# Channels in blocks of 128 and 64 instead of 96 and 96, and an expert stage that alternates up and down products

## The reference

```python
h = tok(x)                                  # sin/cos features of 3*192 inputs, times W -> (4, 512, 192)
h = concat([cls_tok, h], axis=1)            # (4, 513, 192)
h = h + attn(layernorm(h))                  # 8 heads with relative positions, then an MLP 192 -> 384 -> 192
h = h + ffn(layernorm(h))

def ffn(x):
    # "attention" over channels: 12 heads of 16 channels, softmax(q @ k) over channels
    a = (w @ v).reshape(B, N, 192) @ W2_w + W2_b
    x = layernorm_global(a + x)             # one mean and one variance over all images, tokens and channels
    scores = x @ r_w + r_b                  # 8 experts; softmax of the mean over tokens, top 2 per image
    hmid = gelu_tanh(x @ fc_w[e] + fc_b[e]) # 192 -> 768
    m = sum over the 2 experts of gate * (hmid @ proj_w[e] + proj_b[e])
    return layernorm_global(m + x)
```

## Time and profile before

| | us |
|---|---|
| median of three runs | 1060.34 |
| lowest, highest | 1058.44, 1064.05 |
| profiled execution | 1069.61 |
| its span, first to last instruction | 1067.8 |
| PE busy | 937.8 (88%) |
| VectorE busy | 716.2 (67%) |
| ScalarE busy | 659.7 (62%) |
| expert products, first start to last end | 905.7 to 1052.5 |

### The profile page before, as it was taken

The page is one execution under the profiler, slowest core; times in us unless marked ns, Lnnn a source line. Parts: engine busy times, 40 slices in busy tenths (PEclk is TensorE's granted clock), DMA queues, the critical chain, the costliest instruction groups (busy, mean ns, idle before and its releaser), DMA issues. The chain is left out here.

```text
span 1067.8 us, 20398 instructions
## 1 busy us (share of the span) xinstructions
PE 937.8 (88%) x6627; PEld 827.4 (77%) x6627; DVE 716.2 (67%) x1655; ACT 659.7 (62%) x1196; POOL 154.4 (14%) x210
## 2 busy tenths in 40 slices
PE   5999999999977998899889988996978984899996
PEld 5899999999965776677568666764967763899996
DVE  7899979899444865597558655974753436465555
ACT  5767747667436875687569756975344423575653
POOL 1000000000010432043204320444600000000000
PEclk9999999999978998999999999998588997899997
DMA  7012100199514971487148714972001112413101
GB/s 251 21 31 82 36 30 34 34 147 143 83 34 130 274 225 50 119 267 224 52 119 273 225 45 119 284 232 69 29 1 30 30 45 75 133 48 96 48 0 59
DMA packets 81547, 112.93 MB, mean 106 GB/s; under 512 B 10669, under 2 KB 42426, under 8 KB 81482
## 3 DMA queue, kind: packets, MB, share of 16 engines
q1 hardware_dynamic: 81482, 112.16, 39.4%
HBM read 61.30 MB, written 47.67 MB: 102 GB/s over the span
## 5 line engine op out<-in xcount | busy, mean ns | idle before, releaser
L390 PE MATMUL psum<-w,feat 128*128 128x192 f32 x960 | 168.5, 331 | 13.9 <-ACT feat L320 10.3
L390 PEld LDWEIGHTS psum<-w,feat 128*128 128x128 f32 x960 | 157.1, 192 | 14.7 <-issue 10.2
L605 POOL TENSOR_SCALAR a_scores<-a_scores,a_inv 112x514 f32<-112x514 f32 (+1 forms) x160 | 112.6, 705 | 295.3 <-DVE a_inv L954 295.1
L939 DVE CUSTOM_DVE_ANT_0 a_scores<-psum,a_bias 112x514 f32<-112x514 f32 (+1 forms) x160 | 109.9, 689 | 49.7 <-PE psum L678 41.6
L827 ACT ACTIVATE a_scores<-a_scores,a_least 112x514 f32<-112x514 f32 (+1 forms) x160 | 116.6, 728 | 13.6 <-DVE a_least L939 12.9
L408 PE MATMUL psum<-w_parts,parts 128*128 128x384 f32 x368 | 113.0, 372 | 3.4 <-DVE parts L222 2.9
L691 PE MATMUL psum<-ident,a_scores 112*112 112x112 f32 (+1 forms) x800 | 102.7, 260 | 13.4 <-DVE a_probsT L949 8.3
L320 ACT ACTIVATE feat<-turn 128x1024 f32<-128x1024 f32 (+1 forms) x60 | 58.4, 974 | 85.7 <-DVE turn L205 52.5
L678 PE MATMUL psum<-a_kh,a_q 128*112 128x258 f32 (+1 forms) x320 | 101.2, 337 | 7.4 <-DVE a_q L909 3.8
L691 PEld LDWEIGHTS psum<-ident,a_scores 112*112 112x112 f32 (+1 forms) x800 | 78.0, 137 | 35.0 <-POOL a_scores L605 18.7
L632 PE MATMUL psum<-h1T,place 96*128 (+3 forms) x320 | 89.7, 420 | 13.5 <-DVEq L902 6.9
(11 more groups left out here) (271 smaller groups left out, 1759.4 us busy)
## 6 DMA issues: line engine op xcount, KB each, us to landing
shear<-a_pos SPq DMA_DIRECT2D x128, 224.9 KB, 3.9
a_bias<-shear SPq DMA_DIRECT2D x128, 224.4 KB, 3.9
shear<-zero SPq DMA_DIRECT2D x20, 448.9 KB, 17.1
e_fc<-in_e_fc_dram SPq DMA_DIRECT2D x16, 336.0 KB, 4.3
x<-in_xT_dram SPq DMA_DIRECT2D x20, 256.0 KB, 2.9
e_proj<-in_e_proj_dram SPq DMA_DIRECT2D x8, 576.0 KB, 5.2
shear<-a_pos SPq DMA_DIRECT2D x32, 130.5 KB
a_bias<-shear SPq DMA_DIRECT2D x32, 130.3 KB
```

The costliest lines, as they stand in the source:

```text
L390: mm = pe.matmul(sums[m][:, 0:D], feat[:, r, j, 0, 128 * m:128 * m + 128], w[:, k, :], start=begins, stop=ends)
L605: pool.tensor_scalar(row, row, inv[0:TILES[g % NT][1], g % TT:g % TT + 1], 1.0, ALU.mult, ALU.mult).then_inc(weighed, 1)
L939: dve.tensor_tensor_reduce(halves(scores[0:r, g % TT, 0:PADL]), psum2(score_pair(g), r), halves(bias[0:r, g % MR, :]), -1.0 / 8, BIG, ALU. ...
```

## The change

Channels lie in a block of 128 and one of 64. `s.yT` is now 128 partitions x image x 3 x 257: pieces 0 and 1 hold channels 0 to 127 of the first and the second token half, and piece 2 holds channels 128 to 191 of the first half on partitions 0 to 63 and of the second half on partitions 64 to 127 (SIDES). Products that contract over the 64 channels use 64 rows of the array for each half; products that make 64 channels use 64 columns of the array for each half. The hosts' layouts of weights follow (`halved`: the 64-row block is there twice).

In the expert stage the products alternate, one hidden block up and one (two blocks earlier, LAG) down; the 64-channel part of the down product is plain float32, from the unsplit weights and `whole`; the hidden bias comes in with the gelu (`fb`); `whole` and `hidden` have six buffers; the raw down weights three. The loops are written out. The tail's `result`, `mixed_values`, `flip2`, `flip3`, `mix_of`, stores and loads and the output's transposes follow the layout.

```diff
-s.yT_place = sb("yT", [128, 2, B, PADL])
-s.yT = s.yT_place[0:DC]
+s.yT = sb("yT", [128, B, 3, HALF])
 ...
# tail
             def mixed_values(b):
                 for c, pair in enumerate((P0, P1)):
                     for w in range(2):
-                        for k in range(2):
-                            mm = pe.matmul(bank[pair[w]][0:DC, 0:HALF], mix[0:DC + k, k, c, :], zT[0:DC + k, k, b, HALF * w:HALF * w + HALF],
-                                           start=k == 0, stop=k == 1)
+                        pe.matmul(bank[pair[w]][0:DC, 0:HALF], mix[:, 0, c, :], zT[:, b, w, :], start=True, stop=False)
+                    for w, side in enumerate(SIDES):
+                        mm = pe.matmul(bank[pair[w]][0:DC, 0:HALF], mix[side, 1, c, :], zT[side, b, 2, :], start=False, stop=True)
                     mm.then_inc(o_done, 1)
...
+                for k in range(2):
+                    for w, side in enumerate(SIDES):
+                        if c == 0:
+                            mm = pe.matmul(bank[place[w]][:, 0:HALF], cw2[:, k, 0:128], o[:, b % 2, k, w, :], start=k == 0, stop=k == 1)
+                        else:
+                            mm = pe.matmul(bank[place][side, 0:HALF], cw2[:, k, 128:D], o[:, b % 2, k, w, :], start=k == 0, stop=k == 1,
+                                           skip_group_check=True)
...
-                    sp.dma_start(scratch[b, DC * L * c:DC * L * (c + 1)].rearrange("(p n) -> p n", n=L), oT[:, b % 2, c, 0:L]).then_inc(stored, 16)
+                    sp.dma_start(across[:, 0:HALF], oT[:, b % 2, c, 0, :]).then_inc(stored, 16)
+                    sp.dma_start(across[:, HALF:L], oT[:, b % 2, c, 1, 1:HALF]).then_inc(stored, 16)
...
# experts, SP: two loads more per image
+                    sp.dma_start(fb[:, b, k], s.d["e_fcb"][bass.ds(e, 1)].rearrange("e p c -> (e p) c")).then_inc(fb_first_in, 16)
...
# experts, PE
+            def up(n):
+                if n >= 2:
+                    pe.wait_ge(gelu_done, n - 1)
+                for t, (pw, px) in enumerate(TERMS):
+                    for w in range(2):
+                        pe.matmul(s.bank[UP[n % 2][w]][:, 0:WIDE], fc_parts[:, k, pw, 0, cols], x[:, b % 2, px, w, :], start=t == 0, stop=False)
+                for t, (pw, px) in enumerate(TERMS):
+                    for w, side in enumerate(SIDES):
+                        mm = pe.matmul(s.bank[UP[n % 2][w]][:, 0:WIDE], fc_parts[side, k, pw, 1, cols], x[side, b % 2, px, 2, :],
+                                       start=False, stop=t == 2)
+            def down(n):
+                for t, (pw, ph) in enumerate(TERMS):
+                    for w in range(2):
+                        mm = pe.matmul(s.bank[OUT0[w]][:, 0:WIDE], proj_parts[:, k, pw, m, :], hidden[:, ph, m, w, :],
+                                       start=m == t == 0, stop=m == HC - 1 and t == 2)
+                for w, side in enumerate(SIDES):
+                    mm = pe.matmul(s.bank[OUT1][side, 0:HALF], proj[:, (n // HC) % RAW, m, 128:D], whole[:, m, w, :],
+                                   start=m == 0, stop=m == HC - 1, skip_group_check=True)
+            for n in range(ITEMS + LAG):
+                if n < ITEMS:
+                    up(n)
+                if n >= LAG:
+                    down(n - LAG)
...
# experts, ScalarE
+            split_fc(0, 1)
+            act.wait_ge(fb_first_in, 16 * TOPK)
+            item(0)
+            split_proj(0)
+            item(1)
...
# output, PE
-                    for c in range(2):
-                        mm = pe.transpose(s.bank[...][:, D * i + DC * c:D * i + DC * c + DC], s.yT[:, c, b, i0:i0 + 128], s.ident[0:DC, 0:DC])
+                    pe.transpose(s.bank[...][:, D * i:D * i + 128], s.yT[:, b, w, cols], s.ident[:, :])
+                    mm = pe.transpose(s.bank[...][:, D * i + 128:D * i + D], s.yT[side, b, 2, cols], s.ident[side, side])
```

More of the change, by code:

```diff
@@ L1402, in _ @@
             result(3, 0, P0)
-            pe.wait_ge(added, 6)
-            result(3, 1, P1)
+            result(3, 1, P1[1])
         @block.scalar
@@ L1942, in _, with normalize @@
+            for p in range(1, PASSES):
+                more = p + 1 < PASSES
+                for m in range(HC):
+                    item(p * HC + m)
+                    if more and m < 2:
+                        split_fc(p + 1, m)
+                    if more and m == 2 and p % TOPK == TOPK - 1:
+                        split_image(p // TOPK + 1)
+                    if more and m == 3:
+                        split_proj(p + 1)
         @block.vector
         def _(dve):
+            def normalize(b):
+                dve.tensor_scalar(s.yT[:, b, 2, :], s.yT[:, b, 2, :], norm.scale[:, 1:2], norm.shift[:, 1:2],
+                                  ALU.mult, ALU.add).then_inc(normed_d, 1)
@@ new lines, in add_out @@
+            def add_out(p):
+                b, k = divmod(p, TOPK)
+                dve.wait_ge(based, 2 * b + 2)
+                if k:
+                    dve.wait_ge(added, 2 * p)
+                for c in range(2):
+                    if c == 0:
+                        dve.wait_ge(out_done, p + 1)
+                        y, made = s.yT[:, b, 0:2, :], s.psum[:, OUT0[0]:OUT0[0] + 2, 0:HALF]
+                    else:
+                        dve.wait_ge(down_done, (p + 1) * HC)
+                        y, made = s.yT[:, b, 2, :], s.bank[OUT1][:, 0:HALF]
+                    dve.scalar_tensor_tensor(out=y, in0=made, scalar=gates[:, b, k:k + 1], in1=y, op0=ALU.mult, op1=ALU.add).then_inc(added, 1)
@@ L2045, in output_phase @@
         block = ctx.enter_context(nc.Block(no_gpsimd_drain=True))
-        where = [(b, j) for b in range(B) for j in range(2)]
+        where = [(b, w) for b in range(B) for w in range(2)]
         @block.vector
```

552 lines of the change are left out of this document (290 added, 262 removed).

## The result

The changed kernel takes 1078.28 us (median of 4 runs, 1071.42 to 1079.42); beside it the kernel before took 1061.84 (4 runs, 1058.44 to 1064.05). The ratio is 1.0121, 95% interval 1.0089 to 1.0153: 1.2% slower, 12.8 us by the ratio, where +13 was forecast. The total is right, though 1078.28 lies at the upper end of the forecast 1066 to 1079 and above its 1073.

A forecast was written before the change was run, and what follows sets the result against it. PE (TensorE), busy 88% of the span, was taken to bound the expert stage alone. Terms 3.8 + 1.0 + 0.8 + 0.4 + 1.0 + 6.0 = +13.0 on 1060.3 gave 1073 us; forecast 1066 to 1079 (chance 0.50), range 1049 to 1091.

The forecast's parts named there:

- Shape and price of the hidden block: Expert loop: 2.26 us of products plus 0.735 for four shape changes, 3.00 against 2.918; x 48 = +3.8 us.
- row pairs side by side: Expert up products: six 64-row products run as 3 pairs, each pair costing one step of 0.1216 us.
- the column pair in two rounds: Expert down products: plain fp32 products with 64 columns of weights take 2 rounds of 0.22 us.
- cheap changes: Rival, expert loop: only leaving a shape paid, -14.2 us, 1052, chance 0.12; nothing paid, 1031, chance 0.08.
- no pairs: Rival, expert loop: row pairs do not run side by side, +13 to +18 us, 1088, chance 0.10.
- three rounds: Rival, expert loop: the column pair takes three rounds, not two, +10.5 us, 1083.5, chance 0.05.
- The addition at the end of a pass: Boundaries between expert passes: no term; PE was taken as busy in all of each pass from the second on.
- First pass: Expert stage: first activation some 1.5 us later, waiting for hidden biases, and more weight bytes: +1.0 us (0 to +3).
- Output stage: Output transposes: shape changes 32 times, 0.73 us a token block at the lower clock, +6 us (+2.5 to +6.5).
- The two norms: Two global norms: each one's two products on PE become two, four times 0.1 in all, +0.4 us.
- Tail: Tail stage, last image's chain through DRAM: mix, mixed values, stores and loads, result, additions and statistics, +1.0 us (-1 to +3).
- End of the experts: After the last expert product: both halves' addition and statistics now follow it, 2.65 us against 1.85, +0.8 us.

The follow-up runs named there:

- Rows apart: Changed kernel with the six 64-row products of each up product issued as three of the first token half, then three of the second: 1076.68 us (one run).

## Why the prediction was right, and where it was not

**Shape and price of the hidden block: right.** 2.98 us against 3.00; 48 x 0.06 = +2.9 for a forecast of +3.8. Both halves of the working hold: row pairs side by side, the column pair in two rounds (0.58 from 1051.23 to 1051.81, with its change), and 0.18 to 0.19 us for a change, measured at three densities. Its two parts are there as well: in the block shown the first row pair begins 0.21 behind the last full product, the second pair 0.23 behind the first, the third 0.12 behind the second. The three rivals that doubted it (cheap changes, no pairs, three rounds) are out by these rows.

**The addition at the end of a pass: missed, +8.3.** The step that failed is the one on the interleaving: I asked what it does to the first pass and to the last, and took the passes between from the earlier trace rows, "PE is busy in all of it": the boundary was put at nothing. Those rows were of an order in which a pass's ups cover the addition. The changed code has the wait (a down product with m = 0 waits for two additions) and VectorE's queue has the split ahead of the addition; I did not ask, of the wait that moved, what VectorE does ahead of it.

**First pass: -0.9 instead of +1.0.** The expert stage less eight steady passes, less the boundaries, is 156.0 - 143.0 - 8.3 = 4.7 and 5.2 us in the two traces of the changed kernel; before it is 146.8 - 140.1 = 6.7 in the first and 5.5 and 5.4 in the others. The later landing of the hidden biases did hold ScalarE back, but by 0.57 us and not 1.5, as its timeline has it:

```profile
903.44 0.69 ACT L1953 ACTIVATE e_whole<-psum,e_fb 128x514 f32<-128x514 f32 x1 [0.57 <-DMA e_fb<-in_e_fcb_dram]
```

That VectorE's wait for e_pb no longer comes ahead of the first hidden block was in the text and not in the sum; that it makes the gain fits TensorE's shorter waits above, and no run tests it alone.

**Output stage: right.** +5.9 for +6; 0.70 us for a token block against 0.73, at the lower clock throughout (granted 0.50 from 1063.1 to 1075.0).

**The two norms: mis-sized, +2.3 instead of +0.4.** A norm makes two sums on PE, and for each it now issues four instructions where it issued two. The second sum of the first norm, in PE's timelines of before and after:

```profile
895.42 0.34 PE L1019 MATMUL psum<-g_spread,g_var_w 96*96 96x8 f32 x2 [1.24 <-DVE g_spread L1035]
```

```profile
887.91 1.02 PE L1026 MATMUL psum<-g_spread,g_var_w 128*128 128x4 f32 x4 [0.92 <-DVE g_spread L1043]
```

The two rows are not at one clock: the one of before ran at 1.00, that of the changed kernel at 0.50, as the first norm did in all ten traces of its layout and in one of the three of before. Rows apart, a kernel of the changed layout, has the first sum of its second norm at 1.00 (PE's timeline):

```profile
1055.69 0.58 PE L1022 MATMUL psum<-g_mean_var,g_mean_w 128*128 128x4 f32 x4 [3.15 <-PEq L1809]
```

Four instructions take 0.58 us there and 0.99 at half clock, where two of before take 0.31 and 0.46 (L1017). So the added ones are 0.27 us a sum, 1.1 for all four sums, at the full clock and 0.53 a sum, 2.1 in all, at half of it; I priced them at 0.1 a sum.

**Tail: +1.0 forecast, -4.0 measured by the means of the table.** Behind the first gram product the +1.0 has +0.9 against it, though the two lengths of that stretch make this a loose agreement. Ahead of it stands -4.9, the gain of the memset, which the diff shows as one changed line among the constants. The prediction speaks of GpSimd nowhere. Put back, the memset gave 4.6 us of it in one trace: 3.35 us on VectorE, of which TensorE waits 1.15 at once; how the rest reaches TensorE is not shown. The clock takes part in it: granted 0.64 over the stretch in that trace, and between 0.66 and 0.76 in the nine, whose code does not differ there. So the 4.9 and the 4.6 are good to a microsecond or two at best.

**End of the experts:** +0.5 for +0.8.

Sum of the pieces: 2.9 + 8.3 - 0.9 + 0.5 + 2.3 + 5.9 - 4.0 = +15.0; the ratio says +12.8 with an interval of 9.4 to 16.2. The hidden block and the output stage, +9.8 forecast and +8.8 measured, were understood. That the total hit was luck: the boundary (+8.3) and the norms (+1.9) were missed, and the tail (-5.0 against its term), the first pass (-1.9, mis-signed) and the hidden block (-0.9) went the other way. A total alone would have taught that all was understood.

## To carry to other kernels

When an order is interleaved, list for each buffer that is handed back at a boundary who frees it and what stands ahead of that call in the freeing engine's queue: a loop that was bound by one engine in its old order need not be in the new one. Changes of array shape cost about the same at each density tried in this loop, so count them and sort the work by shape (two blocks at a time, an image's flips at a time): with the wait at the boundary gone, the idea lost 0.4% with 4 changes a block, won 1.3% with 1.5, and 2.2% with the flips sorted too. Each of these has the memset's gain in it, some 0.4% by the one trace. And look at what a change takes off the engines that do not count, since a long instruction of GpSimd on a single partition can hold VectorE.

## What was not expected of the hardware

- Products of 64 rows do not have to be issued by turns to run side by side: issued as three of the upper rows and then three of the lower, they still begin in pairs within 0.01 us, three steps for six. A record does not say which half it belongs to; that a product whose rows are free passed two that waited for theirs is how I read three steps for six.
- A change between a full product and a 64-row or 64-column one costs 0.19 us at the full clock, and it is the same between products of one kind in a regular loop: 3.75, 2.98 and 2.53 us for a block with 8, 4 and 1.5 of them.
- One memset of one partition and 4112 values, 3.52 us on GpSimd, made a VectorE scaling of 192 columns last 3.66 us instead of 0.31, in all four traces that have it and in none of the nine that do not.
- The same code from the first gram product to the first norm took 108.7 to 109.4 us in six traces and 112.8 to 113.1 in four (with that of the memset put back), with nothing between, and a single trace on either side cannot be compared there.
